# Two transformer layers on one core: the last feed-forward's ternary weights are quantised during the second layer's attentions

## The reference

```python
def ternary_quant(w_fp32, g=64):
    w = w_fp32.astype(jnp.bfloat16)
    w_g = w.reshape(-1, g)
    scale = jnp.clip(jnp.mean(jnp.abs(w_g), axis=-1, keepdims=True), 1e-08, None)
    q = jnp.clip(jnp.round(w_g / scale), -1, 1)
    w_hat = (q * scale).reshape(w.shape)
    return w + jax.lax.stop_gradient(w_hat - w)
...
    gu = jnp.einsum('bsd,hd->bsh', x, ternary_quant(w_gate_up))      # w_gate_up: 4096 x 512
    gate, up = jnp.split(gu, 2, axis=-1)
    hn = rms_norm(jax.nn.silu(gate) * up)
    return jnp.einsum('bsh,dh->bsd', hn, ternary_quant(w_proj))      # w_proj: 512 x 2048
```

## Time and profile before

| | us |
|---|---|
| median of three runs | 3414.42 |
| profiled execution | 3422.34 |
| its span, first to last instruction | 3420.6 |
| second layer's attentions (two) | about 1600 to 2150 and 2280 to 2830 |
| last feed-forward, first load to last projection | 2893.6 to 3368.3 |
| TensorE busy in the span | 2878.7 (84%) |
| VectorE, ScalarE, GpSimd busy | 1944.4, 1184.9, 942.8 |
| mean granted TensorE clock | 0.927 |

### The profile page before, as it was taken

How to read it: one execution, slowest core, us unless ns; L and a number is a source line. 1 busy time by engine, 2 the same in 40 slices (tenths; PEclk the granted TensorE clock), 3 DMA queues, 4 the chain that set the end, 5 groups by cost and what they waited for, 6 DMA issues and landing times. The chain is left out here.

```text
span 3420.6 us, 42283 instructions
## 1 busy us (share of the span) xinstructions
PE 2878.7 (84%) x14636; PEld 2300.5 (67%) x14636; DVE 1944.4 (57%) x3582; ACT 1184.9 (35%) x2287; POOL 942.8 (28%) x664
## 2 busy tenths in 40 slices
PE   7968888778999997358999999489999993588994
PEld 6846566556888885237888888468888882466773
DVE  5647777582223323345666666556666666766755
ACT  2226555532111111132444444224444442233331
POOL 1226666651111112104000000240000002277633
PEclk9979999988999998689999999799999996799997
DMA  4764333121100001760000000300000003111002
GB/s 171 238 190 123 112 106 110 48 99 56 37 19 19 18 1 64 245 270 27 22 21 32 21 32 17 151 27 22 21 32 21 32 17 135 37 37 37 0 1 98
DMA packets 123391, 236.96 MB, mean 69 GB/s; under 512 B 12832, under 2 KB 67104, under 8 KB 122496
## 3 DMA queue, kind: packets, MB, share of 16 engines
q1 hardware_dynamic: 123264, 235.32, 20.7%
HBM read 162.14 MB, written 72.88 MB: 69 GB/s over the span
## 5 line engine op out<-in xcount | busy, mean ns | idle before, releaser
L1067 POOL TENSOR_TENSOR l0a_probs_hl<-l0a_probs,l0a_probs_hl 128x896 fp32r<-128x896 f32 (+1 forms) x128 | 285.8, 2242 | 161.5 <-ACT l0a_probs L995 161.5
L1299 PE MATMUL l1a_obank<-l1a_pT_hl,l1k_v_hl 128*128 128x512 f32 (+3 forms) x1152 | 300.4, 370 | 7.2 <-DVE l1a_pT_hl L1372 7.1
L1372 DVE TENSOR_TENSOR l1a_pT_hl<-l1a_work,l1a_pT_hl 128x512 fp32r<-128x512 f32 (+3 forms) x384 | 213.1, 555 | 155.1 <-ACT l1a_pT_hl L1332 154.9
L1325 ACT ACTIVATE l1a_probs<-l1a_scores,l1a_row 128x128 f32<-128x128 f32 (+7 forms) x256 | 189.3, 741 | 318.0 <-DVE l1a_row L1362 318.0
L1279 PE MATMUL l1a_scores<-l1k_kT_hl,l1a_qa_hl 128*128 128x512 f32 (+3 forms) x1152 | 291.8, 362 | 1.5 <-ACT l1a_probs L1325 1.5
L1415 POOL TENSOR_TENSOR l1a_q_stage<-l1k_qpe,l1a_ones 128x512 fp32r<-128x512 f32 x32 | 33.3, 1040 | 875.9 <-PE l1a_work L1307 818.4
L1704 DVE TENSOR_TENSOR f0f_hid<-f0f_silu,f0f_ubank 128x512 f32<-128x512 f32 x64 | 44.1, 689 | 319.6 <-PE f0f_ubank L1639 319.6
L1332 ACT CAST l1a_pT_hl<-l1a_work 128x512 fp32r<-128x512 f32 (+3 forms) x384 | 183.5, 478 | 107.3 <-PE l1a_work L1290 106.1
L1307 PE MATMUL l1a_work<-l1a_wov,l1a_oT_hl 128*128 128x512 f32 x768 | 214.1, 401 | 5.0 <-DVE l1a_oT_hl L1391 3.0
L1362 DVE TENSOR_REDUCE l1a_row<-l1a_scores 128x1 f32<-128x128 f32 (+7 forms) x256 | 189.8, 751 | 44.7 <-PE l1a_scores L1282 44.6
L1759 POOL TENSOR_TENSOR f0f_h_hl<-f0f_hid,f0f_h_hl 128x512 fp32r<-128x512 f32 x64 | 82.7, 1292 | 475.6 <-ACT f0f_h_hl L1676 475.6
(11 more groups left out here) (258 smaller groups left out, 6255.3 us busy)
## 6 DMA issues: line engine op xcount, KB each, us to landing
v_dram<-l0f_v_rows SPq DMA_DIRECT2D x24, 768.0 KB, 4.3
qk_dram<-l0f_stage SPq DMA_DIRECT2D x128, 128.0 KB, 2.5
l1a_wov<-wov_dram SPq DMA_DIRECT2D x32, 512.0 KB, 3.4
l0a_v_stage<-v_dram SPq DMA_DIRECT2D x32, 384.0 KB, 4.3
l1a_wabs<-wabs_dram SPq DMA_DIRECT2D x32, 384.0 KB, 3.8
l0a_q_stack<-qk_dram SPq DMA_DIRECT2D x32, 256.0 KB, 3.5
l0a_k_stack<-qk_dram SPq DMA_DIRECT2D x32, 256.0 KB, 3.9
wov_dram<-w1a_wov SPq DMA_DIRECT2D x16, 512.0 KB, 3.3
```

Of the source, the lines that this page charges most:

```text
L1067: nc.gpsimd.tensor_tensor(probs_hl[:, r, 1, 0:wide], probs[:, r, 0:wide], f32(probs_hl[:, r, 0, 0:wide]), ALU.subtract).then_inc(low_done, 1)
L1299: last = pe.matmul(obank[:, c:SPAN], src["v_hl"][:, a, n, :], pT_hl[:, ring(n, s), b, c:SPAN], start=(n == 0 and i == 0), stop=(n == QT * ...
L1325: nc.scalar.activation(probs[s][:, first:first + wide, :].rearrange("p k c -> p (k c)"), scores[:, n % S_AHEAD, 0:wide * P], ACT.Exp, bias ...
L1372: nc.vector.tensor_tensor(pT_hl[:, r, 1, c:SPAN], work[:, slot, c:SPAN], f32(pT_hl[:, r, 0, c:SPAN]), ALU.subtract).then_inc(work_free[slo ...
```

## The change

The quantisation leaves the last feed-forward. The two weight matrices are cut into 48 tiles of 128x512, 24 for each of the two attentions, three for each turn. A tile has a step "A" at the head of its unit (1, 2 and 3 of a turn), ahead of the unit's first "T", and a step "L" in its middle. Cast, sums and comparisons are on the same engines as before; all products and sums of the quantising are GpSimd's. SP loads the float32 tile and stores the bfloat16 one into `gate_up_q` and `down_q` in memory. SP's loop over the heads is written out: in each turn the weights of two heads, and then for each of the turn's three tiles the store and the load of the tile three later. The last feed-forward loads bfloat16 and turns it at once; its groups have no "A" and no "L", and its first group no special order. The diff, cut:

```diff
+CHUNK_OF_UNIT = {1: 0, 2: 1, 3: 2}
+CHUNKS = len(CHUNK_OF_UNIT)
 def unit_events(u, last_unit):
...
+    if u in CHUNK_OF_UNIT:
+        ev.append(("A", h, s, CHUNK_OF_UNIT[u]))
     for kt in range(QT * (s + 1)):
+        if u in CHUNK_OF_UNIT and kt == QT * (s + 1) // 2:
+            ev.append(("L", h, s, CHUNK_OF_UNIT[u]))
         ev.append(("T", h, s, kt))
...
 def attention_layer1(nc, m, ident, ident_bf, mask, src, out, chunks):
...
+    raw = m.sb("raw", [P, CHUNKS, D])
+    wb, ratio, lower, level, diff, quant = (m.sb(n, [P, CHUNKS, D], BF16) for n in (
+        "wb", "ratio", "lower", "level", "diff", "quant"))
...
     def _(sp):
+        def load(h):
+            par = h % 2
+            if h >= 2:
                 sp.wait_ge(x_high, 2 * (h - 1))
+            sp.dma_start(f32(wabs[:, par]), src["wabs_dram"][h]).then_inc(wabs_loaded[par], 16)
+            if h >= 2:
                 sp.wait_ge(o_high, 2 * h - 1)
+            sp.dma_start(f32(wov[:, par]), src["wov_dram"][h]).then_inc(wov_loaded[par], 16)
+        def load_chunk(c):
+            if c >= CHUNKS:
+                sp.wait_ge(cast_done, c - CHUNKS + 1)
+            sp.dma_start(raw[:, c % CHUNKS, :], chunks[c][0]).then_inc(raw_loaded[c % CHUNKS], 16)
+        def store_chunk(c):
+            sp.wait_ge(quant_done, c + 1 + CHUNKS)
+            sp.dma_start(chunks[c][1], quant[:, c % CHUNKS, :]).then_inc(quant_stored[c % CHUNKS], 16)
+        load(0)
+        load(1)
+        for c in range(CHUNKS):
+            load_chunk(c)
+        for turn in range(turns):
+            if turn + 1 < turns:
+                load(HB * turn + 2)
+                load(HB * turn + 3)
+            for c in range(CHUNKS * turn, CHUNKS * (turn + 1)):
+                store_chunk(c)
+                if turn + 1 < turns:
+                    load_chunk(c + CHUNKS)
...
     def _(act):
+                elif kind == "A":
+                    act.wait_ge(raw_loaded[n], 16 * (it + 1))
+                    act.wait_ge(quant_done, seen["A"] + 1)
+                    nc.scalar.copy(wb[:, n, :], raw[:, n, :]).then_inc(cast_done, 1)
...
     def _(dve):
+                elif kind == "A":
+                    dve.wait_ge(cast_done, seen["A"] + 1)
+                    nc.vector.tensor_reduce(total[:, n, :], in_groups(wb, n), AX.X, ALU.add,
+                                            apply_absolute_value=True).then_inc(q_step, 1)
...
+                    nc.vector.reciprocal(inverse[:, n, :], scale[:, n, :]).then_inc(inverse_made, 1)
+                elif kind == "L":
+                    dve.wait_ge(ratio_done, seen["L"] + 1)
+                    nc.vector.tensor_scalar(lower[:, n, :], ratio[:, n, :], -0.5, None, ALU.is_lt).then_inc(lower_done, 1)
+                    dve.wait_ge(lower_done, seen["L"] + 1)
+                    nc.vector.scalar_tensor_tensor(out=level[:, n, :], in0=ratio[:, n, :], scalar=0.5, in1=lower[:, n, :],
+                                                   op0=ALU.is_gt, op1=ALU.subtract).then_inc(level_done, 1)
...
     def _(pool):
+                elif kind == "A":
+                    pool_wait(inverse_made, seen["A"] + 1)
+                    nc.gpsimd.tensor_tensor(in_groups(ratio, n), in_groups(wb, n), per_group(inverse, n), ALU.mult
+                                            ).then_inc(ratio_done, 1)
+                elif kind == "L":
+                    pool_wait(level_done, seen["L"] + 1)
+                    nc.gpsimd.tensor_tensor(in_groups(ratio, n), in_groups(level, n), per_group(scale, n), ALU.mult
+                                            ).then_inc(l_step, 1)
...
+                    nc.gpsimd.tensor_tensor(quant[:, n, :], wb[:, n, :], diff[:, n, :], ALU.add).then_inc(quant_done, 1)
...
-def first_ternary_group():
-
-def each_group(eng, ternary, run):
+def each_group(eng, run):
...
-    raw = m.sb("raw", [P, 2, 3, WC])
+    raw = m.sb("raw", [P, 2, 3, WC], F32 if ternary is None else BF16)
...
-                elif kind == "A":
-                    act.wait_ge(loaded[half], 48 if b else 48 * (it + 2))
-                    act.wait_ge(quant_done, seen["A"] + 1)
-                    nc.scalar.copy(wb[:, :], raw[:, half, a, :]).then_inc(cast_done, 1)
...
+    gate_up_q, down_q = dram("gate_up_q", [2 * HID, D], BF16), dram("down_q", [D, HID], BF16)
+    tiles_of = lambda x: [x[o:o + P, c:c + D] for o in range(0, x.shape[0], P) for c in range(0, x.shape[1], D)]
+    chunks = list(zip(tiles_of(a["L1_ffn_w_gate_up"]) + tiles_of(a["L1_ffn_w_proj"]), tiles_of(gate_up_q) + tiles_of(down_q)))
...
+                                         chunks[b * len(chunks) // B:(b + 1) * len(chunks) // B])
...
+                    feed_forward(nc, m, ident, xT, acc, gate_up_q[0:HID], gate_up_q[HID:2 * HID], down_q,
                                  (ident_bf, squares))
```

More of the change, by code:

```diff
@@ L1223, in _ @@
     def _(sp):
-        def load(h, par, ready=None):
-            if ready is not None:
+        def load(h):
+            par = h % 2
+            if h >= 2:
                 sp.wait_ge(x_high, 2 * (h - 1))
-            sp.dma_start(f32(wabs[:, par]), src["wabs_dram"][bass.ds(h, 1)].rearrange("o p a k c -> p (o a) k c")
-                         ).then_inc(wabs_loaded[par], 16)
-            if ready is not None:
+            sp.dma_start(f32(wabs[:, par]), src["wabs_dram"][h]).then_inc(wabs_loaded[par], 16)
+            if h >= 2:
                 sp.wait_ge(o_high, 2 * h - 1)
[L1231 to L1237, removed]
+            sp.dma_start(f32(wov[:, par]), src["wov_dram"][h]).then_inc(wov_loaded[par], 16)
[18 more added lines that the diff above has]
+                    load_chunk(c + CHUNKS)
+        for i in range(CHUNKS):
+            sp.wait_ge(quant_stored[i], 16 * (turns + 1))
     @block.tensor
@@ L1403, in _ @@
         pool.wait_ge(ones_set, 1)
+        pool.sem_inc(quant_done, CHUNKS)
+        for i in range(CHUNKS):
+            pool.sem_inc(quant_stored[i], 16)
         def pool_wait(sem, value):
@@ L1434, with group_events @@
 WBANKS = 3 * HT
-def group_events(half, turn_next=True, quantise_after=False, first=False, last=False):
+def group_events(half, turn_next=True, first=False, last=False):
     ev = []
@@ L1452, in group_events @@
     return ev + ([("D", half, SPANS - 1, t) for t in range(QT)] if last else [])
-def quantised(half):
-    return [(k, half, w, True) for w in range(3) for k in "AL"]
-def first_ternary_group():
[L1462 to L1473, removed]
-def each_group(eng, ternary, run):
[L1478 to L1482, removed]
+def each_group(eng, run):
+    kinds = "HKDW"
+    opening = [("W", 1, i, 0) for i in range(WBANKS)]
+    first = group_events(0, first=True) + group_events(1)
+    body = group_events(0) + group_events(1)
     tail = group_events(0) + group_events(1, turn_next=False, last=True)
@@ L1567, in bank_view @@
         return wbank[:, i % 2, 0:SPAN].rearrange("p (c h) -> p c h", c=KT)
[L1569 to L1588, removed]
     block = m.ctx.enter_context(nc.Block())
@@ L1652, in run @@
                     last.then_inc(y_full, 1)
-        each_group(pe, ternary is not None, run)
+        each_group(pe, run)
     @block.scalar
@@ L1760, in run @@
                                             ALU.subtract).then_inc(h_low, 1)
-                elif kind == "A" and not b:
-                    make_ratio(pool, nc.gpsimd, seen["A"])
-                elif kind == "L" and not b:
-                    turned = WBANKS * (2 * it + half + 1)
-                    make_quantised(pool, nc.gpsimd, half, a, seen["L"], turned)
-        each_group(pool, ternary is not None, run)
+        each_group(pool, run)
 def scale_rows(nc, m, squares, acc):
```

88 lines of the change are left out of this document (29 added, 59 removed).

## The result

| | before | after |
|---|---|---|
| median, us | 3417.88 (4 runs, 3412.55 to 3423.49) | 3459.22 (4 runs, 3456.64 to 3460.68) |
| ratio to before | | 1.012 (95% interval 1.010 to 1.014) |
| span of the profiled execution | 3420.6 | 3454.9 |
| first attention: first `wabs` load to the next phase's first load | 558.2 | 625.2 |
| second attention, the same | 558.0 | 625.9 |

The change makes the kernel slower, by 41 us in the median and 34 us between the two profiled spans. The last feed-forward gives back 99.6 us, and the two attentions take 134.9 us more. The rest of the span is 1.0 us shorter: the first attention starts 2.8 us earlier, and the stretches behind the attentions and behind the feed-forward are 0.5 to 0.7 us longer each.

A forecast was written before the change was run, and what follows sets the result against it. It took TensorE to bound the attentions, and quantising waits to slow the last feed-forward. Boundaries 97 plus other tiles 34 less feed-forward 97 gave +34 us on the 3420.6 us span, median 3448, range 3388 to 3482.

The forecast's parts named there:

- Feed-forward: Last feed-forward, freed of quantising: gives back 97 us together, bounds 90 and 101.
- The opening: Start of the last feed-forward: with bfloat16 weights the first gate matmul starts at 2905 instead of 2932.5, 27.5 us gained.
- The stop at the turn's end: 14 turn boundaries of the attentions: TensorE stands 5.4 us each for the late load of the next turn's first tile.
- Clock: TensorE behind each turn-boundary stop: part of the next work at 1.2 GHz, 1.5 us lost each (0 to 1.7).
- Units 3: Third unit of each attention turn: first product late by 0.7 us plus 0.3 us beside GpSimd's staging, 16 x 1.0 us.
- Units 2: Second, short unit of each attention turn: VectorE's chain makes the first maximum start later, 16 x 1.0 us.
- Step "L" at nothing: Middle of attention units: 0.29 + 0.69 us on VectorE is covered, 0; without cover 1 us for each of 48.
- GpSimd's lock: Attention units 1 and 3: VectorE blocked by GpSimd's staging, 0.3 us taken; bound 1.0 us more in 18 places, 18 us.
- The cheap boundary: Rival for turn boundaries: load lands in about 2 us, stop 3.9 us without clock loss; 3406 us; 0.14 below 0.3%.
- the boundary in time: Rival for turn boundaries: the load comes in time after all, 48 against 97, -49 us, 3365; chance 0.06.
- The dear one: Rival for turn boundaries: landing in 5.2 us, clock lost in full, 8.8 us each, +78 us, 3492; chance 0.10 beyond range.
- The rival by which units 2 and 3 cost nothing: Rival in the attentions: only the boundary costs, 97 - 97 = 0, 3414 us; 0.10 shared with another rival's near end.

The follow-up runs named there:

- experiment 1: Changed kernel with only SP's order altered: loads of the next three tiles issued as soon as their buffers are cast, ahead of stores and head weights; 3364.12 us, ratio 0.983.
- experiment 2: Changed kernel with, at the turn's end on SP, the three stores first, then the three loads, the first tile's last; 3494.31 us, ratio 1.0209.
- experiment 3: Changed kernel without VectorE's and GpSimd's quantising steps in the attentions; loads, casts and stores stay, cast weights are stored; 3426.26 us, ratio 1.0007.
- Experiment 5: On top of experiment 1, GpSimd's staging of the query moved behind the tile's step "A" in units 1 and 3; 3356.46 us, ratio 0.9803.
- Experiment 4: On top of experiment 1, the tile's cast, sums and comparisons moved inside their units to where VectorE and ScalarE idled; 3335.3 us, ratio 0.9741.
- experiment 6: Changed kernel with its own SP order and only the moved tile steps of Experiment 4; 3331.94 us, ratio 0.9742.

## Why the prediction was right

The mechanism was the forecast one: SP's order makes the load of the turn's first tile late, TensorE stands for it and its clock falls. On the span 34 us were predicted and 34.3 measured, but a match that close is luck: the feed-forward gave 2.6 us more than summed up, the attentions took 3.9 us more, and 1.0 us went elsewhere. In the median it was 41 us, to 3459 where 3448 was predicted; the profiled execution of before lay 4.5 us over its median, that of after 2.6 us under its own, and the spread between executions of one kernel (11 us in before) is not explained here.

- **Feed-forward, 97 us expected, 99.6 measured.** The control inside the trace held: 45.48 us for a full group (45.52 taken), 43.6 for the first (43.7). The opening gave 29.2 instead of 27.5 because the first loads landed for TensorE 5.3 us after their issue, under the 7.2 that I carried over from the larger ones.
- **The stop at the turn's end, 5.4 us expected.** The first product came 7.44 us after the last `wov` (1710.49 - 1703.05), where it had been 1.90 us (1707.04 - 1705.14): 5.54 us later. The cast began 3.97 us after the load's issue (4.2 is the median landing of all such loads), where I took 3.5, but the chain from ScalarE's cast to the product took 2.63 us (1707.86 to 1710.49), under the 2.84 summed up, and the order of issues was 0.1 us quicker. This is one of the cheaper ends; over the twelve it is 5.8 us in the mean (5.5 to 6.4), so the term was 0.4 us too small at each. Experiments 1, 2 and 3 take the wait away, lengthen it and keep it alone.
- **Clock, 1.5 us expected, 1.9 in the mean.** Units 1 and 2 were 8.59 us longer. Less 5.54 for the stop and 0.71 for unit 2 (1.76 less 1.05, experiment 1) that leaves 2.3 us for this end of a turn. The next one (1780.05 to 1821.54, 41.49 us, product 5.76 us later) leaves 1.3. Over the twelve it is 1.2 to 2.8 us, 1.9 in the mean; my bound of 1.7 came from a single stall of 4.07 us. No run took the clock away by itself, but the granted clock accounts for this rest. Below are the 6.8 us behind four of the stops:

```profile
1710.40:1717.20 6.80, 6.71 (x22) 5.43 (x23) 4.04 (x10) 2.61 (x8) 0.67 (x1) 0.61 0.00 0
1787.70:1794.50 6.80, 6.79 (x29) 5.54 (x30) 4.62 (x10) 2.98 (x9) 0.59 (x1) 0.77 0.00 0
1941.50:1948.30 6.80, 6.73 (x29) 5.47 (x30) 4.68 (x11) 3.05 (x9) 0.65 (x1) 0.78 0.00 0
2535.50:2542.30 6.80, 6.74 (x21) 5.50 (x22) 4.01 (x10) 2.57 (x8) 0.64 (x1) 0.54 0.00 0
```

  TensorE is busy nearly throughout. The share of the clock that is missing, times 6.8 us, is 2.7, 1.6, 1.5 and 3.1 us (an estimate of the time lost), and the rests at these four ends are 2.3, 1.3, 1.2 and 2.8 us. They rise and fall together, while the stops themselves (5.16, 5.38, 5.45 and 5.28 us) do not. Three matmuls took 1.65 us at the first product where 0.94 was usual.
- **Units 3, 1.0 us expected, 1.05 measured, for the reasons given:** 0.7 us by the chain and 0.4 us by GpSimd's staging (0.3 taken). Experiment 5 shows the second part. **Units 2, 1.0 expected, 0.71 taken from experiment 1,** on the assumption that its units 1 cost as much as its units 3: the third block of scores waited 0.53 us only, since the maximum had stood 0.29 us for the scores before and now follows right behind the low part.
- **Step "L" at nothing** held. Unit 3's first product in the changed kernel:

```profile
1748.40 0.94 PE L1337 MATMUL l1a_obank<-l1a_pT_hl,l1k_v_hl 128*128 128x512 f32 x3 [0.80 <-DVE l1a_pT_hl L1414]
```

  It comes 3.08 us behind the `wov` of 1745.32, 1.18 us later than the 1.90 of before, and units 3 and 4 are 1.05 us longer: the late product covers the whole loss, and "L" in the middle of the unit adds nothing. Experiment 4 moved "L" as well, so it doesn't bear on this.
- **GpSimd's lock.** The Trainium skill (SBUF — State Buffer, on the shared port pair) says that, of a GpSimd instruction and a VectorE instruction in a two-port mode, the one that starts second is blocked until the first ends. The trace agrees in that the mean ended with GpSimd's instruction; that the mean runs in such a mode no run shows. It had begun 0.57 us before that end and took 0.58, so the cost was 0.41 us over its own 0.17; the bound of 1.0 us took the whole staging step for what was left of it, and was too wide.
- **Rivals.** The cheap boundary (3406) and the boundary in time (3365) fell with the 71.5 us of ScalarE's waits. The dear one (3492) has the time that experiment 2 gave (3494), by another sum: its own premise, a landing of 5.2 us, did not come (4.2 in the median). The rival by which units 2 and 3 cost nothing (3414) fell with their 0.71 and 1.05 us.
- **A slip without effect.** The prediction calls the attentions two stretches of about 590 us; they are 558 us each. No term uses it.

## What to carry to other kernels

Before work is moved into a stage that a busy engine bounds, ask two things of each new step in the strict order of its engine: what stands behind it on the way to the busy engine's next instruction, and by how much that came early until now. A load belongs as far ahead of its use as the longest wait queued before it on the issuing engine, or its use has to move back by as much; either cure removed the whole stop here. Filling idle time by an engine's busy share misleads: the same instructions and the same loads cost 135 us with the steps at the heads of the units and 8 us a few steps further on (experiment 6).

## What the runs showed of the hardware

- In the changed kernel each of TensorE's 14 stops, 5.1 to 6.0 us long, was followed by three matmuls in 1.62 to 1.65 us where 0.94 was usual, at 1.2 GHz where I read the granted clock. What the clock cost was not constant: 1.3 us at one end of a turn and 2.3 us at another, with stops of 5.38 and 5.16 us.
- A VectorE instruction of 0.17 us on 8 columns took up to 0.59 us beside a GpSimd instruction on SBUF and ended with it. Beside the same staging, VectorE's low part with one operand in PSUM took its usual 0.68 us, and so did the sum of absolute values, with its one bfloat16 input in SBUF (1742.75 in experiment 1, 0.68 us; 0.68 in unit 2 without a neighbour).
- Loads of the same 256 KB tiles landed in 4.2 us (median) where three of them went out right behind 512 KB of weights with stores between them, and in 2.8 us in experiment 4, where they went out some 7 us behind the weights. Of the last feed-forward's bfloat16 loads of 256 KB, those of `gate_up_q` landed in 2.8 us and those of `down_q` in 3.6.
